# Mamba layers on one core: the residual add moved to POOL, the scan's DMA order and tile steps rearranged, and the layer norm's root issued later

## The chip, the cores and the metric
The kernel runs on one core of a Trainium2 chip. The metric is the device time of one execution in microseconds (us). Engines: PE (TensorE), DVE (VectorE), ACT (ScalarE), POOL (GpSimd), and SP, which only issues DMAs here.

## What is computed
Four layers are applied one after the other to x of shape (4, 1024, 512), float32. Layer 0 is softmax attention, layer 1 linear attention; the change leaves them alone. Layers 2 and 3 are Mamba blocks with a gate from the conditioning vector (layer 3 works on rows permuted by an index):

```python
xn = _layernorm(x, ln_g, ln_b) * (1.0 + scale[:, None, :]) + shift[:, None, :]
xz = xn @ in_proj.T                 # x_in and z, 1024 columns each
u  = silu(causal_conv4(x_in))
dt_r, B, C = split(u @ x_proj.T, [64, 80])
dt = softplus(dt_r @ dt_proj.T + dt_b)
h  = h * exp(dt_t * A) + (dt_t * u_t) * B_t      # for each time step t, 1024 x 16 states
y  = sum_n(h * C_t) + u * D
out = x + gate[:, None, :] * ((y * silu(z)) @ out_proj.T)
```

## The kernel before, in words
The program is one launch with a block for each stage; in a block each engine has its own queue, in an order written out by hand, and semaphores between the queues. Each of the two Mamba layers has two stages.

**ssm_inputs** handles the four batches in turn (loop `it`). For a batch PE makes the x products (8 tiles m of 128 channels), DVE does the convolution, ACT the silu; then come the x_proj product and its copy to SBUF by ACT (`proj_copy`), and then a loop over m = 0 to 7: PE makes one z product (z_with(m)) and DTP(m), DVE takes `relu(m)` of DTP, ACT its `Abs`. ACT works in two groups of four m: behind the fourth Abs of a group it loads the table of Exp, does four Exp, loads the table of Ln and does four Ln; DVE's `finish_dt(m)` needs the Ln. Between the groups, at m = 4, PE makes four more z products (Z_MID), and behind each of them `turn_rows(it + 1, ...)`: four transposes of the next batch's centered rows. These rows are centered by DVE (`rows.center`, eight steps, a semaphore after the fourth and the eighth), which waits for `rows.root` on ACT: Ln and Exp of the variances, on a 128x8 tile. DVE's queue has relu(0) to relu(3), center(it + 1), finish_dt(0), finish_dt(1), relu(4), finish_dt(2), ... PE uses a ring of four PSUM banks for z products and turned rows, which ACT empties (`take_z` with silu, `take_rows`).

**scan** runs over 64 blocks: 4 batches x 2 halves of 512 time steps x 8 channel tiles m. A block has 8 units of two states n; a unit k is two DVE scans (`recur`), with `h` held in a ring of three groups of four units. Around a unit:
- PE `make_drive(k + 4)` makes the input terms, ACT `lay(k + 4)` copies them into h;
- ACT `decay(k)` makes exp(dt * A) for both states, DVE `recur(k)` scans;
- POOL `multiply(k)` multiplies the two states by C, held in Crep (16 states x 512 steps, in four quarters of 1 MB; one buffer, reloaded at each change of half);
- PE `turn(k - 2)` transposes and sums over states into y; behind a block's last unit the u * D term follows, then DVE `gate` multiplies by silu(z) in zg, and SP stores it to scratch g.

The output products of 32 tiles of 128 rows are woven in, 16 units per tile, a half behind the scan: `tile_at(k)` gives the tile and the step within it. PE transposes g (`turn_g`, two parts, from og), ACT copies (`copy_g`), PE makes 8 `product`s into the bank O, DVE `gate_o` multiplies by the gate; in layer 2 a second DVE instruction adds the residual x. Layer 3 has residual None and adds it later, in gather_add. O, og, o and x have one buffer each.

SP's queue issues, per block, the loads of uD, dT, B, z, dt, og, x, gt and the stores of g and o, each with its wait. At the last block of a half (m = 7) it also reloads Crep: `load_C(half, q)` waits until POOL has done 2q + 2 units of that block.

In the code below these names stand as they are; a first half (th = 0) starts its scans from zero, a second half (th = 1) from `carry`.

## Time and profile before

| | us |
|---|---|
| median of 3 runs | 7161.26 (7154.28 to 7166.18) |
| the profiled execution, its own time | 7161.26 |
| its span, first to last instruction | 7159.3 |
| ssm_inputs of layer 2 / scan of layer 2 | about 2850 to 3600 / 3605 to 4975 |
| ssm_inputs of layer 3 / scan of layer 3 | about 4975 to 5730 / 5730 to 7078 |

Times in rows are microseconds from the span's start unless marked ns. A row of a timeline has the start, the duration, the engine, the line of the kernel, the operation and out<-in; x8 means eight merged instructions, and the bracket tells how long the engine was idle before and what released it. Instructions on one engine overlap a little, so a pitch is read from start to start.

### The profile page before, as it was taken

To read this page: it belongs to the slowest core of one execution; us is meant where nothing else is said; L and a number is where in the kernel's file an instruction comes from. 1 tells how busy PE (TensorE), PEld (TensorE's weight loads), DVE (VectorE), ACT (ScalarE), POOL (GpSimd) and SP (SyncE) were. 2 spreads that over 40 slices of the span, in tenths; PEclk is the share of its full clock that TensorE was granted. 3 is DMA by queue.
4 is the path that set the end of the run, shared out by engine and by line. 5 is a ranking of instruction groups with operands and counts; after the bars stand their busy time and mean duration, and the time that the engine had idled before them with its cause. 6 is when DMAs were issued, how large, how long until landed. Compare 5 with 4: busy or idle time off the path is not lost. (4 is left out here: it accounts for less than half of the span.)

```text
span 7159.3 us, 89203 instructions
## 1 busy us (share of the span) xinstructions
PE 5975.5 (83%) x31488; PEld 4036.9 (56%) x31488; DVE 5018.3 (70%) x6369; ACT 4537.6 (63%) x6817; POOL 2482.0 (35%) x1098
## 2 busy tenths in 40 slices
PE   6989999999889757988858888886888768888883
PEld 2448888888634343434356666663344356666661
DVE  2459999999642244454489999994454489999992
ACT  1228888888621142444479889993455489999991
POOL 0000000000000000000079999993000089999993
PEclk9999999999989878999889999998999889999996
DMA  5442222222242244233356666553233456655554
GB/s 196 170 150 60 72 63 74 66 72 60 87 147 97 111 148 173 87 140 132 149 147 164 166 159 159 155 157 100 99 135 129 152 148 167 159 154 156 151 146 169
DMA packets 608855, 935.18 MB, mean 131 GB/s; under 512 B 104984, under 2 KB 252568, under 8 KB 607908
## 3 DMA queue, kind: packets, MB, share of 16 engines
q1 hardware_dynamic: 596964, 904.27, 42.0%
q0 software_dynamic: 5120, 16.78, 0.7%
q10 hardware_dynamic: 6336, 8.52, 0.3%
q8 instruction: 249, 4.08, 0.2%
q14 instruction: 186, 1.52, 0.1%
HBM read 590.40 MB, written 338.98 MB: 130 GB/s over the span
## 5 line engine op out<-in xcount | busy, mean ns | idle before, releaser
L1609 POOL TENSOR_TENSOR scan_hC<-scan_h,scan_Crep 128x1024 f32<-128x1024 f32 x1024 | 2395.0, 2376 | 2880.7 <-DVE scan_h L1776 2856.2
L1720 ACT ACTIVATE scan_a<-scan_dt,scan_A 128x512 f32<-128x512 f32 x2048 | 1371.1, 696 | 117.7 <-DVE scan_h L1776 94.1
L1643 PE MATMUL scan_y<-ident,scan_hC 128*128 128x128 f32 x8192 | 1116.3, 280 | 384.1 <-POOL scan_hC L1609 383.1
L1643 PEld LDWEIGHTS scan_y<-ident,scan_hC 128*128 128x128 f32 x8192 | 902.7, 142 | 781.1 <-POOL scan_hC L1609 705.7
L1776 DVE TENSOR_TENSOR_SCAN scan_h<-scan_a,scan_carry,scan_h 128x512 f32<-128x512 f32 x1024 | 1214.6, 1260 | 13.7 <-ACT scan_a L1720 13.7
L1776 DVE TENSOR_TENSOR_SCAN scan_h<-scan_a,scan_h 128x512 f32<-128x512 f32 x1024 | 1155.3, 1200 | 55.8 <-ACT scan_a L1720 53.4
L1696 ACT COPY scan_h<-scan_drive 128x1024 f32<-128x1024 f32 x1024 | 1040.8, 1016 | 146.8 <-PE scan_drive L1631 137.1
L1631 PE MATMUL scan_drive<-scan_Bd,scan_dT 128*128 128x256 f32 x4096 | 751.8, 306 | 117.0 <-ACT scan_h L1696 57.6
L805 DVE TENSOR_TENSOR att_pTlo<-att_TP,att_pThi 128x512 fp32r<-128x512 f32 x1024 | 657.9, 684 | 128.1 <-ACT att_pThi L843 126.3
L843 ACT CAST att_pThi<-att_TP 128x512 fp32r<-128x512 f32 x1024 | 547.8, 587 | 179.7 <-PE att_TP L738 172.5
L1631 PEld LDWEIGHTS scan_drive<-scan_Bd,scan_dT 128*128 128x128 f32 x4096 | 560.0, 193 | 163.5 <-issue 78.1
L798 DVE CUSTOM_DVE_ANT_0 att_sm<-att_S,att_mneg 128x1024 f32<-128x1024 f32 x512 | 622.0, 1215 | 12.3 <-POOL att_mneg L716 12.1
L858 ACT ACTIVATE att_pr<-att_sm,att_nmax 128x1024 f32<-128x1024 f32 x512 | 592.4, 1157 | 45.9 <-DVE att_nmax L798 45.9
L738 PE MATMUL att_TP<-ident,att_pr 128*128 128x128 f32 x4096 | 564.9, 278 | 25.0 <-DVE att_pTlo L805 24.8
L497 PE MATMUL p_bank<-p_W,p_xT 128*128 128x512 f32 x1280 | 566.6, 599 | 5.1 <-ACT p_xT L395 5.1
L738 PEld LDWEIGHTS att_TP<-ident,att_pr 128*128 128x128 f32 x4096 | 452.4, 141 | 184.8 <-issue 116.8
L746 PE MATMUL att_YT<-att_pThi,att_v 128*64 128x256 f32 x2048 | 538.5, 298 | 0.0
L1669 PE MATMUL scan_O<-scan_Wo,scan_gT 128*128 128x512 f32 x1024 | 533.6, 614 | 5.4 <-ACT scan_gT L1727 5.4
L1205 PE MATMUL ssmin_ring<-ssmin_Wz,ssmin_xT 128*128 128x512 f32 x1024 | 476.4, 614 | 46.9 <-ACT ssmin_zt L1275 46.9
L746 PE MATMUL att_YT<-att_pTlo,att_v 128*64 128x256 f32 x2048 | 496.5, 277 | 0.0
L716 POOL TENSOR_SCALAR att_mneg<-att_mrow 128x1024 f32<-128x1024 f32 x4 | 14.5, 3636 | 1267.1 <-DMA att_mrow<-mask 1267.1
L1205 PE MATMUL ssmin_ring<-ssmin_xT,ssmin_Wx 128*128 128x512 f32 x1024 | 452.9, 598 | 0.0
(151 smaller groups left out, 6828.6 us busy)
## 6 DMA issues: line engine op xcount, KB each, us to landing
scan_dT<-scratch_dtuT SPq DMA_DIRECT2D x512, 256.0 KB, 5.5
scratch_dtuT<-ssmin_dT SPq DMA_DIRECT2D x128, 512.0 KB, 2.9
scan_Crep<-scratch_bc SPq DMA_DIRECT2D x64, 1024.0 KB, 9.6
att_q<-scratch_q_split SPq DMA_DIRECT2D x256, 128.0 KB, 3.0
att_k<-scratch_k_split SPq DMA_DIRECT2D x256, 128.0 KB, 3.2
scratch_uD<-ssmin_uD SPq DMA_DIRECT2D x64, 512.0 KB, 4.4
scratch_z<-ssmin_zt SPq DMA_DIRECT2D x128, 256.0 KB, 2.0
scratch_dt<-ssmin_dt SPq DMA_DIRECT2D x64, 512.0 KB, 2.6
```

The costliest lines, as they stand in the source:

```text
L738: last = nc.tensor.transpose(TP[:, m * P:(m + 1) * P], pr[u % 2][:, m * P:(m + 1) * P], ident[:])
L746: last = nc.tensor.matmul(YT[:, pair * 2 % 4:pair * 2 % 4 + 2, :], v[n // 4 % 2][:, m, n % 4, :].bitcast(F32R), pT[part][pair % 2][:, :, m ...
L798: nc.vector.tensor_tensor_reduce(sm[u % 2][:], S[u % 2][:], mneg[b % 2][:], -1.0, HUGE, ALU.add, ALU.min, nmax[u % 2][:]).then_inc(s["shif ...
L805: nc.vector.tensor_tensor(pT[1][u // 2 % 2][:, u % 2, cols_].bitcast(F32R), TP[:, cols_], pT[0][u // 2 % 2][:, u % 2, cols_], ALU.subtract ...
L858: nc.scalar.activation(pr[u % 2][:], sm[u % 2][:], ACT.Exp, bias=nmax[u % 2][:, 0:1], scale=-1.0, accum_out=psums[:, at:at + 1]).then_inc( ...
L1205: last = nc.tensor.matmul(ring[e % 4][:], lhs, rhs, start=(kt == 0), stop=(kt == KT - 1))
L1609: nc.gpsimd.tensor_tensor(hC[k % 2][:], of, Crep[:, 2 * p:2 * p + 2, :], ALU.mult).then_inc(s["scaled"].handle, 1)
L1631: last = nc.tensor.matmul(drive[:, c * TC:(c + 1) * TC, :], dT[j][:, at * P:(at + 1) * P].bitcast(F32R), Bd[th][:, at, :, first:first + GS ...
L1643: last = nc.tensor.matmul(y[j][:, t, :], hC[k % 2][:, i, t * P:(t + 1) * P], ident[:], start=(p == 0 and i == 0 and t == 0), stop=False, i ...
L1696: nc.scalar.copy(h[group % 3][:, :, tt * P:(tt + 1) * P], drive[:].rearrange("p t n -> p n t")).then_inc(s["laid"].handle, 1)
L1720: nc.scalar.activation(a[(2 * k + i) % 3][:], dt[j][:], ACT.Exp, scale=A[:, m, 2 * p + i:2 * p + i + 1]).then_inc(s["decayed"].handle, 1)
L1776: nc.vector.tensor_tensor_scan(of, a[(2 * k + i) % 3][:], of, first, ALU.mult, ALU.add).then_inc(s["scanned"].handle, 1)
```

## The change
In ssm_inputs, `rows.root(act, it + 1)` moves from behind proj_copy to behind the first group's Ln. In scan:
- the residual add of layer 2 moves from DVE (out of PSUM) to POOL (from o and x, both in SBUF), with a semaphore o_added;
- the tile's steps: start 4 units into the half instead of 8; turn_g's second part at step 5 (was 4), the products at 7 to 14 (were 6 to 13), gate_o at 15 (was 13); the loops end earlier;
- in PE's queue, turn(k - 2) comes ahead of turn_g and product of the same k;
- SP's order: load_C's four quarters all go last in the block of m = 7, x and the first part of og go behind z in odd blocks, the o store and og's second part into even blocks, around z.

```diff
                 nc.scalar.copy(xd[:], X[0:R + 2 * NS, :]).then_inc(c["proj_copy"].handle, 1)
-                if it + 1 < B:
-                    rows.root(act, it + 1)
                 for group in (range(0, 4), range(4, 8)):
                     if group[0] == 4:
+                        if it + 1 < B:
+                            rows.root(act, it + 1)
                         for n in Z_MID:
                             take_z(n)
...
-            n = (k - HALF_UNITS - UNITS) // 16
-            return (n, (k - HALF_UNITS - UNITS) % 16) if 0 <= n < TILES else (None, None)
+            n = (k - HALF_UNITS - 4) // 16
+            return (n, (k - HALF_UNITS - 4) % 16) if 0 <= n < TILES else (None, None)
...
             def load_C(half, q):
                 b, th = half // 2, half % 2
-                if half:
-                    w(sp, "scaled", half * HALF_UNITS - UNITS + 2 * q + 2)
...
-            for blk in range(BLOCKS + IB + 2):
+            for blk in range(BLOCKS + IB + 1):
                 half, m = blk // IB + 1, blk % IB
-                tile = (blk - IB - 1) // 2
+                tile = (blk - IB) // 2
                 if blk < BLOCKS:
                     load_uD(blk)
-                if m % 2 == 1 and 0 <= tile < TILES:
-                    load_og(tile, 1)
-                    if tile % TT == 0:
-                        load_gt(tile)
-                if m % 2 == 1 and 1 <= tile <= TILES:
-                    store_o(tile - 1)
-                if m % 2 == 0 and 0 <= tile < TILES and residual is not None:
-                    load_x(tile)
-                change = half < 2 * B and m == IB - 1
-                if change:
-                    load_C(half, 0)
                 if blk + 2 < BLOCKS:
                     load_dT(blk + 2)
-                if change:
-                    load_C(half, 1)
                 if half < 2 * B and 1 <= m <= 4:
                     load_B(half, range(8 * (m - 1), 8 * m))
                 if 1 <= blk <= BLOCKS:
                     store_g(blk - 1)
...
+                if m % 2 == 0 and 1 <= tile <= TILES:
+                    store_o(tile - 1)
                 if blk < BLOCKS:
                     load_z(blk)
-                if change:
-                    load_C(half, 2)
-                if m % 2 == 1 and 0 <= tile + 1 < TILES:
-                    load_og(tile + 1, 0)
+                if m % 2 == 0 and 0 <= tile < TILES:
+                    load_og(tile, 1)
+                if m % 2 == 1:
+                    if 0 <= tile < TILES:
+                        if tile % TT == 0:
+                            load_gt(tile)
+                        if residual is not None:
+                            load_x(tile)
+                    if 0 <= tile + 1 < TILES:
+                        load_og(tile + 1, 0)
                 if blk + 2 < BLOCKS:
                     load_dt(blk + 2)
-                if change:
-                    load_C(half, 3)
+                if half < 2 * B and m == IB - 1:
+                    for q in range(4):
+                        w(sp, "scaled", blk * UNITS + 2 * q + 2)
+                        load_C(half, q)
...
+            def add_residual(n):
+                w(pool, "o_gated", n + 1)
+                pool.wait_ge(x_in.handle, x_in.at(16 * (n + 1)))
+                nc.gpsimd.tensor_tensor(o[:], o[:], x[:], ALU.add).then_inc(s["o_added"].handle, 1)
+
+            for k in range(UNITS_ALL + HALF_UNITS + 8):
+                if k < UNITS_ALL:
+                    multiply(k)
+                n, step = tile_at(k - 2)
+                if residual is not None and step == 15:
+                    add_residual(n)
...
                 if k + 4 < UNITS_ALL:
                     make_drive(k + 4)
+                if 0 <= k - 2 < UNITS_ALL:
+                    turn(k - 2)
                 n, step = tile_at(k)
                 if step == 1:
                     turn_g(n, 0)
-                if step == 4:
+                if step == 5:
                     turn_g(n, 1)
-                if step is not None and 6 <= step < 14:
-                    product(n, step - 6)
-                if 0 <= k - 2 < UNITS_ALL:
-                    turn(k - 2)
+                if step is not None and 7 <= step < 15:
+                    product(n, step - 7)
...
-                if residual is None:
-                    nc.vector.tensor_tensor(o[:], O[:], gt[:], ALU.mult).then_inc(s["o_gated"].handle, 1)
-                else:
-                    nc.vector.tensor_tensor(O[:], O[:], gt[:], ALU.mult).then_inc(core.vector_step.handle, 1)
-                    dve.wait_ge(core.vector_step.handle, core.vector_step.at(n + 1))
-                    dve.wait_ge(x_in.handle, x_in.at(16 * (n + 1)))
-                    nc.vector.tensor_tensor(o[:], O[:], x[:], ALU.add).then_inc(s["o_gated"].handle, 1)
+                nc.vector.tensor_tensor(o[:], O[:], gt[:], ALU.mult).then_inc(s["o_gated"].handle, 1)
...
                 n, step = tile_at(k - 1)
-                if step == 13:
+                if step == 15:
                     gate_o(n)
```
On ACT copy_g's second part moves from step 5 to step 6.

## Rows read from the trace of the kernel before

**Rows 1.** Busy time by window; columns PE, PEld, DVE, ACT, POOL, PEclk, DMA share, GB/s
```profile
3640.00:4895.00 1255.00, 1027.96 (x6923) 806.60 (x6923) 1225.74 (x1123) 1135.12 (x1623) 1175.57 (x504) 0.99 0.58 154
...
4990.00:5725.00 735.00, 631.93 (x1696) 289.81 (x1696) 340.74 (x389) 351.13 (x434) 23.29 (x24) 0.91 0.35 127
```

**Rows 2.** Timeline of ACT, ssm_inputs of layer 3, batch 0
```profile
5093.41 0.30 ACT L367 ACTIVATE ssmin_lv<-ssmin_mv,eps 128x8 f32<-128x8 f32 x1
5093.73 1.28 ACT L370 ACT_TABLE_LOAD   x1
5095.02 0.21 ACT L370 ACTIVATE ssmin_rstd<-ssmin_lv 128x8 f32<-128x8 f32 x1
...
5115.06 1.11 ACT L1320 ACTIVATE ssmin_ea<-ssmin_DTP,column_tables 128x1024 f32<-128x1024 f32 x1 [2.71 <-DVE ssmin_dt L1380]
...
5126.98 1.28 ACT L1275 ACT_TABLE_LOAD   x1
```

**Rows 3.** Timeline of PE, the same stretch
```profile
5117.10 0.60 PE L387 MATMUL ssmin_ring<-ident,ssmin_x 128*128 128x128 f32 x4
5117.53 3.60 PE L1205 MATMUL ssmin_ring<-ssmin_Wz,ssmin_xT 128*128 128x512 f32 x8
5120.97 0.60 PE L387 MATMUL ssmin_ring<-ident,ssmin_x 128*128 128x128 f32 x4
5128.92 6.12 PE L1205 MATMUL ssmin_ring<-ssmin_Wz,ssmin_xT 128*128 128x512 f32 x8 [7.36 <-ACT ssmin_zt L1275]
...
5143.15 1.98 PE L1238 MATMUL ssmin_DTP<-ssmin_xd,ssmin_Wdt 64*128 64x512 f32 x4
```

**Rows 4.** Timeline of DVE, the same stretch
```profile
5114.94 3.73 DVE L377 TENSOR_SCALAR ssmin_x<-ssmin_x,ssmin_mv,ssmin_rstd 128x512 f32<-128x512 f32 x8
```

**Rows 5.** Groups by line, 4990 to 5725: busy us, mean ns, idle before
```profile
L1205 PE MATMUL ssmin_ring<-ssmin_Wz,ssmin_xT 128*128 128x512 f32 x512 | 238.4, 614 | 23.4 <-ACT ssmin_zt L1275 23.4
```

**Rows 6.** Timeline of DVE, gate_o of successive tiles, in three stretches of the scans
```profile
4028.06 0.67 DVE L1761 TENSOR_TENSOR scan_O<-scan_O,scan_gt 128x512 f32<-128x512 f32 x1
...
4066.46 0.68 DVE L1761 TENSOR_TENSOR scan_O<-scan_O,scan_gt 128x512 f32<-128x512 f32 x1
...
4149.49 0.68 DVE L1761 TENSOR_TENSOR scan_O<-scan_O,scan_gt 128x512 f32<-128x512 f32 x1
...
4189.62 0.67 DVE L1761 TENSOR_TENSOR scan_O<-scan_O,scan_gt 128x512 f32<-128x512 f32 x1
...
6118.40 0.67 DVE L1759 TENSOR_TENSOR scan_o<-scan_O,scan_gt 128x512 f32<-128x512 f32 x1
...
6156.07 0.67 DVE L1759 TENSOR_TENSOR scan_o<-scan_O,scan_gt 128x512 f32<-128x512 f32 x1
```

**Rows 7.** Timeline of POOL, a first half of layer 2
```profile
3969.16 23.28 POOL L1609 TENSOR_TENSOR scan_hC<-scan_h,scan_Crep 128x1024 f32<-128x1024 f32 x10 [0.38 <-DVE scan_h L1776]
```

**Rows 8.** Waits in the scans: us in total, times, longest; layer 2 twice, then layer 3
```profile
DVE scan_o L1764 <- DMA scan_x<-scratch_x: 17.9, 6, 3.8
...
DVE scan_h L1776 <- ACT scan_a L1720: 9.6, 8, 1.9
...
DVE scan_h L1776 <- ACT scan_a L1720: 13.8, 10, 3.2
```

**Rows 9.** SP's issue of dt in a block; then all landings of Crep
```profile
4066.24 0.33 SPq L1504 DMA_DIRECT2D scan_dt<-scratch_dt  x1
...
DMA to landing us min/median/max: 5.8/9.6/14.3
```

**Rows 10.** Timeline of POOL and DVE behind a change of half, layer 3
```profile
6705.94 6.97 POOL L1609 TENSOR_TENSOR scan_hC<-scan_h,scan_Crep 128x1024 f32<-128x1024 f32 x3 [3.13 <-DMA scan_Crep<-scratch_bc]
...
6713.06 2.34 DVE L1776 TENSOR_TENSOR_SCAN scan_h<-scan_a,scan_h 128x512 f32<-128x512 f32 x2 [3.19 <-ACT scan_a L1720]
6717.21 4.57 DVE L1776 TENSOR_TENSOR_SCAN scan_h<-scan_a,scan_h 128x512 f32<-128x512 f32 x4 [1.81 <-ACT scan_a L1720]
```

**Rows 11.** Timeline of PE behind the last scan of layer 2
```profile
4900.85 3.60 PE L1669 MATMUL scan_O<-scan_Wo,scan_gT 128*128 128x512 f32 x8
```

More of the change, by code:

```diff
@@ L1456, in scan @@
                                                   "y_full", "gated", "A_in")}
-        s.update({"o_" + n: core.count("out_" + n) for n in ("turned", "copied", "made", "gated")})
+        s.update({"o_" + n: core.count("out_" + n) for n in ("turned", "copied", "made", "gated", "added")})
         crep_in = core.slot_in[0:4]
@@ L1465, in scan @@
         where = lambda blk: (blk // (2 * IB), blk // IB % 2, blk % IB)
+        o_done = s["o_gated" if residual is None else "o_added"]
         def tile_at(k):
-            n = (k - HALF_UNITS - UNITS) // 16
-            return (n, (k - HALF_UNITS - UNITS) % 16) if 0 <= n < TILES else (None, None)
+            n = (k - HALF_UNITS - 4) // 16
+            return (n, (k - HALF_UNITS - 4) % 16) if 0 <= n < TILES else (None, None)
         block = ctx.enter_context(nc.Block())
@@ L1534, in load_x @@
                 if n >= 1:
-                    w(sp, "o_gated", n)
+                    w(sp, "o_added", n)
                 sp.dma_start(x[:], residual[n // TT, n % TT * P:(n % TT + 1) * P, :]).then_inc(x_in.handle, 16)
@@ L1544, in store_o @@
             def store_o(n):
-                w(sp, "o_gated", n + 1)
+                sp.wait_ge(o_done.handle, o_done.at(n + 1))
                 sp.dma_start(dst[n // TT, n % TT * P:(n % TT + 1) * P, :], o[:]).then_inc(o_out.handle, 16)
@@ L1610, in multiply @@
                                         ).then_inc(s["scaled"].handle, 1)
-            for k in range(UNITS_ALL):
-                multiply(k)
+            def add_residual(n):
[8 more added lines that the diff above has]
+                    add_residual(n)
         @block.tensor
@@ L1674, in _ @@
                 make_drive(n)
-            for k in range(UNITS_ALL + HALF_UNITS + UNITS + 2):
+            for k in range(UNITS_ALL + HALF_UNITS + 8):
                 if k + 4 < UNITS_ALL:
                     make_drive(k + 4)
+                if 0 <= k - 2 < UNITS_ALL:
+                    turn(k - 2)
                 n, step = tile_at(k)
@@ L1731, in _ @@
                 lay(n)
-            for k in range(UNITS_ALL + HALF_UNITS + UNITS + 2):
+            for k in range(UNITS_ALL + HALF_UNITS + 8):
                 if k < UNITS_ALL:
@@ L1741, in _ @@
                     copy_g(n, 0)
-                if step == 5:
+                if step == 6:
                     copy_g(n, 1)
@@ L1782, in _ @@
                                       ).then_inc(s["cleared"].handle, 1)
-            for k in range(UNITS_ALL + HALF_UNITS + UNITS + 2):
+            for k in range(UNITS_ALL + HALF_UNITS + 8):
                 if k < UNITS_ALL:
@@ L1800, in scan @@
     if residual is not None:
-        core.vector_step.stage_added(TILES)
+        s["o_added"].stage_added(TILES)
         x_in.stage_added(16 * TILES)
```

## The prediction
> **What bounds the kernel now.** I read the busy time by stage first [rows 1]. In layer 2's scan DVE is busy for 1225.74 of 1255 us (98%) and POOL for 1175.57 (94%). In the stage ahead of layer 3's scan, which prepares its inputs, no engine is full: PE has 631.93 of 735 us. So in a scan what DVE does sets the time and POOL is 4% behind it, while in the input stage one must look at which wait ends last. For that I read the ACT and PE timelines of one batch's middle, then the tiles' pitch on DVE in the scans, then the waits and SP's issues where the scan changes half.
>
> **The change, part by part**, against the profiled execution (span 7159.3, time 7161.26, which is also the median of the three runs; the 2 us between them stay).
>
> *1. rows.root moved behind the first Exp/Ln group.* Today ACT does the root (Ln, table load, Exp) right after proj_copy and is through at 5095.2 [rows 2]. It costs nothing there: PE's Z products wait nowhere but in the stall below (0 otherwise [rows 5]), and ACT's fourth Abs (5115.06) waits 2.71 us on DVE's relu, not on ACT's own earlier work [rows 2]. So leaving it out there gains nothing. In its new place it starts at 5126.98, where the next silu table load starts today. Ln needs no new table (Ln has just run): 0.30; table load 1.28; Exp 0.21: root done at 5128.8 instead of 5095.2; the silu table then comes at 5130.1, in time for a ring bank that PE needs only after its next product. On DVE, center is queued ahead of finish_dt(0); today it starts at 5114.94 and does 8 steps in 3.73 us [rows 4]. Then it starts at 5128.85, and its first four steps (the first half, which PE waits for) end about 1.95 us later, at 5130.8. PE has turn_rows(it+1, 0) queued directly behind the first Z_MID product; today it runs at 5117.10, the second product at 5117.53 and its turn at 5120.97, all under ACT's Exp/Ln [rows 3]. Afterwards PE stands at the first turn until 5130.8, and those three come behind it.
> Today from the end of that stall (5128.92) to DTP(4) (5143.15) are 14.23 us, with third and fourth Z_MID products, z_with(4) and their turns, the first product at a fallen clock (6.12 us instead of 3.60). After the change a turn (0.43), a product (3.44) and a turn (0.43) come ahead of these 14.23, all from 5130.85 on: 5130.85 + 4.30 + 14.23 = 5149.38, so 6.23 us later. All after DTP(4) (relu and Abs of m = 4 to 7, second Exp/Ln, finish_dt, next batch's x products) hangs on it: nothing in that chain has spare work to hide it. The stall today occurs three times in the layer (23.4 us [rows 5]), that is once for each batch with a root behind it, and 2 x 3 = 6 in the kernel: 6 x 6.23 = **+37.4**. Bounds: 33 (if PE's restart costs a little less) to 46 (if the doubled idle time, 13.6 us instead of 7.36, makes it restart 1.4 us slower).
> The Trainium skill (ScalarE: Activation LUTs, section "Table sets: the hidden batching unit") has Ln and Exp in one common set, so that Exp behind Ln needs no load. Here the trace disagrees: a load of 1.28 us stands between them [rows 2]. By the rule each root would end 1.28 us earlier and the part would come to +29.7.
>
> *2. The residual add moves from DVE to POOL (layer 2 alone).* Tile pitch on DVE in a first half (scan from zero) is 4066.46 - 4028.06 = 38.40 us, in a second half 40.13; layer 3, which has no add, has 37.66 in a first half [rows 6]. So DVE gains 38.40 - 37.66 = 0.74 us per tile. POOL does ten multiplies in 23.28 us [rows 7], a pitch of (23.28 - 2.36) / 9 = 2.32, or 37.2 per tile of 16. An add of 128x512 on POOL stands nowhere in the trace; the nearest row is this multiply of twice the size, 2.36 us. Upper end 2.36 (no less for half the size), lower 0.69 (DVE's own add, as layer 3's lack of it shows 0.74); I take half the multiply, 1.18, plus a little: 1.2. In first halves POOL then needs 38.4, as much as today's DVE pitch, so the 12 tiles there gain nothing (+0.2 each for the uneven load: 2.4). In second halves DVE keeps 39.39 against POOL's 38.4 to 38.8, but the add delays the multiply behind it by 1.1 us and PE, ACT and DVE are linked tightly (three units of scan between a multiply and the scan that its turn lets go), so I give 0.45 back: -0.29 x 15 tiles = -4.4. Sum **-2**; with 0.69: -17; with 2.36: +14.
> The Trainium skill (GPSIMD Engine Reference, section "3.1 Elementwise — side-by-side cycle accounting") gives 4497 ns for a two-input add of 2048 elements. An estimate from that page with the 2.36 of this trace for 1024 puts 512 elements at 1.3 us; it would add about 1.2 us to the sum.
>
> *3. SP's order: the four Crep loads go last, x goes earlier.* Today DVE waits 17.9 us for x in six tiles, all behind a change of half, because x sits behind Crep; DVE also waits 9.6 us (layer 2) and 13.8 us (layer 3) for scan_a, nearly all just behind changes, where a late Crep or og held PE [rows 8]. The new order issues z, x and og ahead of Crep. If all of it goes: 17.9 + 9.6 + 13.8 = **-41**.
> The price: the first Crep quarter used to go out six units of scan ahead of its use. Now it stands behind load_dt(blk+2), which waits for the block's last decay. Such an issue stands at 4066.24, 0.2 us before the end of the seventh scan unit (4066.46) [rows 6, 9]. With one unit (2.3) left in the block, dt goes out 2.5 us and Crep 2.0 us ahead of the new half; POOL needs it one unit in, 4.3 us after issue. Landings of Crep are 5.8 at least, 9.6 in the middle, 14.3 at most [rows 9]; the 5.8 belongs to a load at the head of a burst, as here, but with up to 1 MB of z, x, og and dt just ahead of it. I take 6.7: POOL stalls 2.4. In the trace a POOL stall of 3.13 on Crep makes DVE lose 3.19, and 1.81 more four units on [rows 10]; in the new PE order a product stands between turn and the next drive, so there is less slack. I price 2.4 at 2.3 of DVE: seven changes in each scan, 14 x 2.3 = **+32**. Bounds: 1.5 of stall, most of it absorbed, 14 x 0.8 = 11; the middle landing 9.6, stall 5.3, 14 x 5 = 70. The later quarters then have room: POOL uses one per 4.6 us.
>
> *4. PE's order and the tile's steps.* turn now precedes the tile's transposes and products, so a product (3.60 / 4 = 0.9 us [rows 11]) lies in the chain turn, drive, lay, decay. In second halves, with 0.1 us more per unit (pitch 39.4 against 37.7 for 16), this fits; in first halves I take 0.15 us for each of layer 3's 12 tiles: **+2** (0 to 6).
>
> *5. The tail.* Four products of tile 27 (3.60 us) follow the last turn today [rows 11]; two would, so the O bank is free 1.8 us earlier. In layer 2 the store ahead of og waits for POOL's add (+0.3 on each of four tiles, +0.6 on the last). Together **-1.5** (-4 to +3).
>
> Sum: 37.4 - 2 - 41 + 32 + 2 - 1.5 = +26.9, so 7161.3 + 26.9 = **7188**.
>
> **The rivals.**
> *A. The Crep burst lands in time* (not slower). POOL would stall no more than today; the point that decides is a landing of 4.3 us or less after issue, or a slack that absorbs the stall. Then the 32 go: 7156. For it: the landing of 5.8 is only 1.5 us over that point. Against: no Crep load of the trace landed below 5.8.
> *B. root's move is hidden*: PE would have other work or the late batch would be caught up before the next one. Then the 37.4 go: 7151. Against: PE's queue is in order, and the stall at 5128.92 is on the one chain that leads to DTP(4).
> *C. The burst is worse than its head*: Crep quarters queue behind each other and behind dT, landings come near the middle of the rows (9.6), and DVE loses 5 per change: 26.9 + 38 = +65, 7226. For it: the 14.3 us landing belongs to the third load of a burst. Against: a first load of a burst landed in 5.8.
> *D. POOL becomes the bound of layer 2*: an add of 2.36 us, +16 over the sum: 7204. For it: POOL has 1.2 us per tile to spare in first halves, no more. Against: multiply's time is mostly elements.
> *E. Exp needs no load behind Ln* (the rule cited in part 1): the root ends 1.28 us earlier six times: 7180. Against: today's load between the two.
>
> **How the numbers follow.** Chances: the forecast 0.60, A 0.13, B 0.06, C 0.11, D 0.08, E 0.02. The time is the forecast's, 7188; its own range is 7172 to 7206. The 8-in-10 range leaves out the far part of C, where 14 x 5 applies at every change, and what lies beyond A and B together: 7152 to 7224. A measurement of this kernel tells 0.2% (14 us) from no change, that is 7147 and 7175.6. Faster: A and B at once, or either with a cheap add: 0.08. Same: the rest of A, B and the low edge of the forecast (0.06 of it): 0.17. Slower: 0.75.
>
> **What would show it.** In the changed profile: PE's wait ahead of the first turn_rows of the next batch should appear at about 13 us, on DVE's center, six times, and the 7.36 us wait on the silu should be gone; the input stages should each be 19 us longer. No x wait on DVE; 32 POOL adds of about 1.2 us; POOL's waits on Crep at the first unit of each half, about 2 us each, 14 times; tile pitch in layer 2 near 38.4 and 39.7. I would be wrong if center ran before the Exp/Ln group, if Crep landed in under 4.5 us or its quarters queued, or if the add took over 1.5 us.

## The result and the profile after

| | us |
|---|---|
| the changed kernel, median of 4 runs | 7287.30 (7279.52 to 7292.78) |
| the kernel before, median of 4 runs beside it | 7158.04 (7154.28 to 7166.18) |
| ratio, with its 95% interval | 1.0178 (1.0161 to 1.0196) |
| profiled execution, its own time / span | 7276.74 / 7274.9 |

The change makes the kernel 1.8% slower, 127 us by ratio. The prediction had the sign right and the size wrong: 7188, with 7224 as its upper end. In the profiled executions the 115.6 us between the spans lie here. A scan is taken from the start of its first DVE scan to the start of its last; an input stage from its first root, or from the end of layer 2's last o, to the first scan; a tail from there to the end of the layer's last o.

| stretch | before | after | difference | forecast |
|---|---|---|---|---|
| ssm_inputs of layer 2 | 760.7 | 780.6 | +19.8 | +18.7 |
| scan of layer 2 | 1276.2 | 1323.0 | +46.8 | about -13 |
| ssm_inputs of layer 3 | 785.7 | 805.2 | +19.5 | +18.7 |
| scan of layer 3 | 1243.5 | 1280.7 | +37.2 | about +4 |
| the two tails | 149.6 | 146.6 | -3.0 | -1.5 |

What lies ahead of layer 2's inputs and behind layer 3's last o, which the change doesn't touch, is 4.0 and 0.7 us shorter. So the input stages came as forecast and the scans did not. First the windows, as in [rows 1] (busy time of PE, PEld, DVE, ACT, POOL, then the clock):

```profile
3656.00:4940.00 1284.00, 1044.60 (x6840) 834.04 (x6840) 1200.06 (x1081) 1119.90 (x1607) 1190.39 (x524) 0.97 0.56 149
5070.00:5800.00 730.00, 625.19 (x1662) 283.67 (x1660) 329.17 (x360) 336.30 (x417) 23.27 (x24) 0.92 0.34 123
```
In layer 2's scan DVE is busy for 93% of the time, before for 98%: it is less full and yet the stage is longer. No engine became the bound by its work (POOL 93%); the engines wait for each other.

**The input stage.** ACT, then PE, in the stretch that answers to [rows 2, 3], and last PE's first Z_MID product before:

```profile
5189.09 1.28 ACT L370 ACT_TABLE_LOAD   x1
```
```profile
5175.48 3.70 PE L1205 MATMUL ssmin_ring<-ssmin_Wz,ssmin_xT 128*128 128x512 f32 x8
5192.69 1.08 PE L387 MATMUL ssmin_ring<-ident,ssmin_x 128*128 128x128 f32 x4 [13.50 <-DVE ssmin_x L377]
5193.56 4.74 PE L1205 MATMUL ssmin_ring<-ssmin_Wz,ssmin_xT 128*128 128x512 f32 x8
...
5210.29 1.98 PE L1238 MATMUL ssmin_DTP<-ssmin_xd,ssmin_Wdt 64*128 64x512 f32 x4
```
```profile
5113.56 3.70 PE L1205 MATMUL ssmin_ring<-ssmin_Wz,ssmin_xT 128*128 128x512 f32 x8
```
The first Z_MID product stands 61.92 us later than before (5113.56). From there the turn comes at 5130.77 on the old time (forecast 5130.85), after a wait of 13.50 on center in place of the 7.36 on the silu table, and DTP(4) 5.22 us later than before (forecast 6.23; the product behind the stall took 4.74, not 6.12). Another 0.86 us comes at PE's next restart after an idle time (its sixteen products take 8.73 us, before 7.88). That is 6.1 us for this batch; the layer's other two batches with a root behind them lose 6.6 and 6.8. The wait of 13.50 stands there in all six. The table load between Ln and Exp is there (1.28).

**The scans.** DVE's gate_o in successive tiles, as in [rows 6]: a first and a second half of layer 2, then of layer 3:

```profile
4346.79 0.68 DVE L1763 TENSOR_TENSOR scan_o<-scan_O,scan_gt 128x512 f32<-128x512 f32 x1
4387.76 0.68 DVE L1763 TENSOR_TENSOR scan_o<-scan_O,scan_gt 128x512 f32<-128x512 f32 x1
...
4139.75 0.68 DVE L1763 TENSOR_TENSOR scan_o<-scan_O,scan_gt 128x512 f32<-128x512 f32 x1
4180.79 0.68 DVE L1763 TENSOR_TENSOR scan_o<-scan_O,scan_gt 128x512 f32<-128x512 f32 x1
...
6205.64 0.68 DVE L1763 TENSOR_TENSOR scan_o<-scan_O,scan_gt 128x512 f32<-128x512 f32 x1
6244.68 0.68 DVE L1763 TENSOR_TENSOR scan_o<-scan_O,scan_gt 128x512 f32<-128x512 f32 x1
...
6367.35 0.68 DVE L1763 TENSOR_TENSOR scan_o<-scan_O,scan_gt 128x512 f32<-128x512 f32 x1
6407.24 0.68 DVE L1763 TENSOR_TENSOR scan_o<-scan_O,scan_gt 128x512 f32<-128x512 f32 x1
```
Before, in a second half of layer 3:
```profile
5963.40 0.67 DVE L1759 TENSOR_TENSOR scan_o<-scan_O,scan_gt 128x512 f32<-128x512 f32 x1
6002.79 0.67 DVE L1759 TENSOR_TENSOR scan_o<-scan_O,scan_gt 128x512 f32<-128x512 f32 x1
```
The pitch is 40.97 and 41.04 in layer 2 (before 38.40 and 40.13) and 39.04 and 39.89 in layer 3 (before 37.67 and 39.39). Over 12 tiles in first and 15 in second halves that is 31 + 14 + 16 + 7 = 68 us. The scans are 84 us longer; the 16 that are left lie where the scan changes half.

The 40.97 is not the pitch of every first-half tile of layer 2. Here are two of them from gate_o to gate_o, with columns as in [rows 1], the third from the right being the granted clock of PE:
```profile
4346.79:4387.76 40.97, 35.13 (x226) 28.06 (x225) 37.99 (x36) 36.33 (x55) 38.52 (x18) 0.96 0.51 131
4641.54:4681.79 40.25, 33.31 (x221) 26.05 (x220) 38.00 (x37) 36.42 (x55) 38.48 (x18) 1.00 0.58 148
```
Away from the changes of half, a tile in a first half of layer 2 has 40.24 to 40.27 where the granted clock was 1.00 and 40.9 to 41.1 where it was 0.96. So some 0.7 us of the 2.57 go with the clock and 1.9 do not. Over layer 2's whole scan the mean granted clock is 0.97, before 0.98.

The add and all landings of Crep, as in [rows 9]:

```profile
L1611 POOL TENSOR_TENSOR scan_o<-scan_o,scan_x x32: 1262/1276/1291, 3850.0 to 5033.8; 128x512 f32<-128x512 f32 x32
```
```profile
  DMA scan_Crep<-scratch_bc: 34.8, 14
...
DMA to landing us min/median/max: 6.1/10.9/18.1
```
The same wait of POOL before:
```profile
  DMA scan_Crep<-scratch_bc: 17.2, 14
```
Both are as priced: an add of 1.28 us, and POOL waits for Crep 14 times for 2.49 (forecast 2.4). Fourteen waits alone would prove little, since before there were 14 too, of 1.2 us; but all of those stood at the third or fourth quarter, and now 13 of the 14 stand at the first quarter of a new half, as forecast. That quarter lands 6.6 to 7.7 us behind its issue (forecast 6.7). The next two do queue behind it, 9.3 to 11.2 and 12.4 to 14.4 us behind theirs, but POOL's only other wait for Crep is 0.2 us. DVE has no wait for x any more. What is new stands in the waits of layer 2's scan, of after and of before:

```profile
ACT scan_h L1701 <- PE scan_drive L1636: 133.0, 153, 6.4
...
DVE scan_h L1775 <- ACT scan_a L1725: 82.4, 65, 5.8
```
```profile
ACT scan_h L1696 <- PE scan_drive L1631: 36.0, 64, 2.9
```
ACT's lay waits for the drive in 153 units instead of 64, and behind it DVE for scan_a 82.4 us instead of 9.6 [rows 8]. So the first theory was PE's order; rivals were the steps and the add.

### The profile page after: what moved, and what is told of

Its sections match the earlier page's. It is cut to its first block and busy times, and to the rows that moved or that the text cites. A ratio compares the mean times of both kernels' runs of the same rounds, so it can differ in the third digit from the quotient of the medians.

```text
span 7274.9 us, 89191 instructions
## 1 busy us (share of the span) xinstructions
PE 6039.8 (83%) x31488; PEld 4103.6 (56%) x31488; DVE 5012.1 (69%) x6337; ACT 4517.0 (62%) x6805; POOL 2521.1 (35%) x1130
## 3 DMA queue, kind: packets, MB, share of 16 engines
q1 hardware_dynamic: 596964, 904.27, 41.1%
## 5 line engine op out<-in xcount | busy, mean ns | idle before, releaser
L1648 PE MATMUL scan_y<-ident,scan_hC 128*128 128x128 f32 x8192 | 1139.6, 283 | 369.5 <-POOL scan_hC L1605 364.5
L1725 ACT ACTIVATE scan_a<-scan_dt,scan_A 128x512 f32<-128x512 f32 x2048 | 1351.9, 694 | 48.6 <-DVE scan_h L1775 45.4
L1636 PE MATMUL scan_drive<-scan_Bd,scan_dT 128*128 128x256 f32 x4096 | 881.4, 338 | 139.6 <-ACT scan_h L1701 84.4
L1636 PEld LDWEIGHTS scan_drive<-scan_Bd,scan_dT 128*128 128x128 f32 x4096 | 600.9, 195 | 414.1 <-issue 249.2
## 6 DMA issues: line engine op xcount, KB each, us to landing
scan_Crep<-scratch_bc SPq DMA_DIRECT2D x64, 1024.0 KB, 10.9
```

Source lines behind the costliest of these rows:

```text
L1636: last = nc.tensor.matmul(drive[:, c * TC:(c + 1) * TC, :], dT[j][:, at * P:(at + 1) * P].bitcast(F32R), Bd[th][:, at, :, first:first + GS ...
L1648: last = nc.tensor.matmul(y[j][:, t, :], hC[k % 2][:, i, t * P:(t + 1) * P], ident[:], start=(p == 0 and i == 0 and t == 0), stop=False, i ...
L1725: nc.scalar.activation(a[(2 * k + i) % 3][:], dt[j][:], ACT.Exp, scale=A[:, m, 2 * p + i:2 * p + i + 1]).then_inc(s["decayed"].handle, 1)
```

## The experiments

All ratios below are to the kernel before on the same chip, with half-intervals of 0.0009 to 0.0019; 0.0014 is 10 us. So a difference between two of these runs is uncertain by 10 to 20 us. "Given back" is counted against the changed kernel.

**One edit undone at a time.** e1 puts turn(k - 2) behind product again, e2 the steps (start at 8 units, second turn_g at 4, products at 6, gate_o and POOL's add at 13), e3 the add, e4 the root.

```diff
# e1
-                if 0 <= k - 2 < UNITS_ALL:
-                    turn(k - 2)
                 n, step = tile_at(k)
...
                     product(n, step - 7)
+                if 0 <= k - 2 < UNITS_ALL:
+                    turn(k - 2)
# e2
-            n = (k - HALF_UNITS - 4) // 16
+            n = (k - HALF_UNITS - UNITS) // 16
...
```

> The changed kernel with one edit undone: in PE's queue turn(k - 2) stands behind turn_g and product again. Theory 1: the tile's pitch grew by 2.57 us (layer 2, first halves, 12 tiles), 0.91 (15 tiles), 1.37 and 0.49 (layer 3), 68 us in all, because each product now lies in the chain turn, drive, lay, decay, scan: ACT's lay waits for the drive in 154 units of layer 2 instead of 65. Then undoing the order gives back 30 to 50 us (time 7237 to 7257), and layer 3's pitch returns to 37.7 and 39.4. Theory 2: the steps are the cause (the gate_o of a tile now falls on the same unit as the block's gate with silu(z), and the first part of the tile on other units). Then this run stays within 10 us of the changed kernel (7277 to 7290) and layer 3's pitch stays at 39.0. Theory 3: it is the add on POOL; then layer 3 has no part in it, and layer 2's pitch of 40.97 stays.

> The changed kernel with the tile's steps undone (start 8 units into the half, second turn_g at 4, products at 6 to 13, gate_o and POOL's add at 13), PE's order and all else as changed. Theory 1 (PE's order is the cause): within 10 us of the changed kernel, 7277 to 7297, the pitch in layer 3's first halves still near 39.0. Theory 2 (the steps are, gate_o and gate on the same unit): 20 to 50 us are given back, 7237 to 7267, and layer 3's pitch falls under 38.2.

> The changed kernel with the residual add back on DVE (two instructions, out of PSUM), all else as changed. Theory 3 (POOL's add of 1.28 us starves the scan of layer 2): 25 to 40 us are given back, 7247 to 7262, and layer 2's pitch falls from 40.97 and 41.04 to under 39.8 and 40.5. Theory 1 (PE's order): DVE has 0.7 us more work per tile but the loss by POOL goes, so between -10 and +10 us, 7277 to 7297. My prediction had it at +2, because it priced the move at -2.

> The changed kernel with rows.root(act, it + 1) back behind proj_copy, all else as changed. The input stages of both layers are 38.7 us longer in the changed profile (19.8 and 18.9); the theory that root's place makes all of it expects 37 to 40 given back, 7247 to 7250, PE's wait for center (85.8 us of DVE for rstd in 8 times) gone and the stall of 7.4 on the silu table back. Rival: part of the 38.7 came from elsewhere (the scan that ends differently, or code loading), then under 30 are given back, above 7257.

| run | median us | ratio |
|---|---|---|
| e1, PE's order undone | 7293.05 | 1.0197 |
| e2, steps undone | 7245.63 | 1.0131 |
| e3, add undone | 7255.73 | 1.0145 |
| e4, root undone | 7236.49 | 1.0116 |

e4: input stages 761.4 and 784.7, 19.2 and 20.5 us shorter, spans 40.9 apart: the root's place makes all of term 1. The median lies 10 us below the expectation's 7247 to 7250, and by ratio 44 us come back. (The 18.9 in the expectation ran from the start of the last o before and from its end after; end to end it is 19.5.)

e1 refutes the plain form of theory 1: no time came back. Yet its pitch in layer 3's first halves is 37.85, as it said, so something else ate it. The PE and SP timelines behind a change of half in e1 show what:

```profile
6181.14 0.71 PE L1636 MATMUL scan_drive<-scan_Bd,scan_dT 128*128 128x256 f32 x4
6186.69 1.11 PE L1666 MATMUL scan_O<-ident,scan_og 128*128 128x128 f32 x4 [4.83 <-DMA scan_og<-scratch_g]
6187.60 1.91 PE L1648 MATMUL scan_y<-ident,scan_hC 128*128 128x128 f32 x8
```
```profile
6183.11 0.37 SPq L1515 DMA_DIRECT2D scan_zg<-scratch_z  x1
6183.58 0.45 SPq L1529 DMA_DIRECT2D scan_og<-scratch_g  x1
```
The new SP order loads og's second part behind z, and the new steps ask for it three units earlier (start 4 and step 5, before 8 and 4); with turn queued behind turn_g, PE stands 4.83 us at og and the scan with it (31.8 us in 7 times in layer 3; 2.4 in the changed kernel). So the change needs its PE order as a guard against its own late og. e6 below completes the square: with the old steps PE's new order costs 57 us (e2 against e6), with the new steps it costs nothing that can be told (the changed kernel against e1, -14); the new steps cost 104 us with PE's old order (e1 against e6) and 34 with the new one.

e2 and e3 both give much back (34 and 24 us by ratio), and both chiefly in layer 2 (scan 1288.8 and 1297.3 against 1323.0). e3 is what theory 3 said in time and nearly in pitch (39.76 and 40.61 in layer 2). e2 is what theory 2 said in time, but layer 3's pitch stays at 38.85 and doesn't fall under 38.2. No single theory says both: the parts interact.

**Parts alone.** e5 has only PE's order changed in the kernel before; e6 is the changed kernel with steps and PE's order undone; e7 is the kernel before with SP's new order; e8 the changed kernel with Crep's four loads issued at their old places:

```diff
# e8
                 if blk < BLOCKS:
                     load_uD(blk)
...
+                if change:
+                    crep(0)
                 if blk + 2 < BLOCKS:
                     load_dT(blk + 2)
+                if change:
+                    crep(1)
...
-                if half < 2 * B and m == IB - 1:
-                    for q in range(4):
-                        w(sp, "scaled", blk * UNITS + 2 * q + 2)
-                        load_C(half, q)
...
```

> The kernel before with one edit of the change: in PE's queue turn(k - 2) ahead of turn_g and product of the same k. The run with the order undone (e1_pe_order) gave no time back, but its pitch in layer 3's first halves was 37.85 against 39.03, and what it won there it lost in a wait of PE for og (31.8 us in 7 times in layer 3). Theory: the order itself costs pitch, and in the kernel before, where og comes in time, nothing is won for it: layer 3's pitch goes from 37.67 to 38.85 and from 39.40 to 39.88 (12 x 1.2 + 15 x 0.5 = 22 us), layer 2's from 38.4 and 40.13 by 0.3 to 1.2: together 25 to 45 us, 7180 to 7200. Rival: pitch grows only together with the add on POOL or the new steps: within 5 us of the kernel before, 7150 to 7160.

> The changed kernel with the tile's steps and PE's order both undone; root's place, the add on POOL and SP's order stay. With the steps undone alone it took 7245.6. Theory (product in the chain is the cause of the rest of the pitch): layer 3's pitch falls from 38.85 to 37.7 and from 39.88 to 39.4 (22 us), layer 2's from 39.4 to about 38.6 and 40.0 to 39.6 (16 us), and og, asked for later now, comes in time: 7200 to 7215. Rival: the wait for og that took the gain in e1_pe_order comes here too, 14 times 4 us: above 7240.

> The kernel before with SP's new order as its only edit (Crep's four quarters last in the block of m = 7, x and og earlier). My prediction: x and scan_a waits go (-41), POOL stalls 2.4 in 14 changes at 2.3 of DVE each (+32): -9, about 7146. Theory from the changed kernel, where the changes of half together cost 2 us more than before in layer 2 and 13 more in layer 3: +15, about 7170. Second theory: part of those 15 comes from the early steps or PE's order, then between: 7150 to 7160.

> The changed kernel with the four loads of Crep issued where the kernel before has them (around dT and z, the last behind dt), all else as changed. Theory: POOL's waits for Crep (34.8 us in 14 changes) and the 3 to 4.5 us that DVE loses behind each go: 25 to 45 us given back, 7245 to 7262. Rival: z, og and x come behind 1 MB loads again, and PE or DVE wait for these instead: within 10 us of the changed kernel, 7277 to 7297.

| run | median us | ratio |
|---|---|---|
| e5, before + PE's order | 7202.93 | 1.0071 |
| e6, changed - steps - PE's order | 7197.45 | 1.0052 |
| e7, before + SP's order | 7145.70 | 0.9981 |
| e8, changed, Crep early | 7257.45 | 1.0141 |

e5: PE's order alone costs 0.7% or 51 us, with nothing else changed, a little more than the 25 to 45 expected; the rival is out. PE in a first half of layer 3, first before, then e5:

```profile
6133.11 1.09 PE L1643 MATMUL scan_y<-ident,scan_hC 128*128 128x128 f32 x8 [0.36 <-POOL scan_hC L1609]
...
6137.22 1.02 PE L1669 MATMUL scan_O<-scan_Wo,scan_gT 128*128 128x512 f32 x2
6138.08 1.04 PE L1643 MATMUL scan_y<-ident,scan_hC 128*128 128x128 f32 x8
6138.87 0.72 PE L1631 MATMUL scan_drive<-scan_Bd,scan_dT 128*128 128x256 f32 x4
```
```profile
6166.38 1.09 PE L1643 MATMUL scan_y<-ident,scan_hC 128*128 128x128 f32 x8 [0.30 <-POOL scan_hC L1609]
6167.31 1.02 PE L1669 MATMUL scan_O<-scan_Wo,scan_gT 128*128 128x512 f32 x2
6167.77 1.03 PE L1631 MATMUL scan_drive<-scan_Bd,scan_dT 128*128 128x256 f32 x4
```
Before, a unit without a product has PE wait 0.36 us for POOL's multiply ahead of turn (6133.11). In a unit with one the product runs at that time, PE doesn't wait, and the drive follows the turn at once. In e5 PE first waits for POOL, then turns, then makes the product, and the drive ends later by the product and takes 1.03 instead of 0.72; ACT's lay waits 0.51 for it in the next unit (6168.89 of its timeline).

e6 lands at 37 us over before by its ratio (interval 24 to 50). The prediction's sum without parts 4 and 5 is +26: so the miss is in the steps, PE's order and what these do to the other parts, as far as an interval of 26 us can tell. e7 refutes the +15 and agrees with the prediction's -9 (measured -14): DVE waits 16.0 and 16.2 us for scan_a in the two scans and never for x, 32.2 in place of 41.3, where -41 and +32 were forecast. e8 is as expected (-26 us by ratio): POOL's Crep waits fall from 34.8 to 4.7, DVE's gain is partly lost to og (PE waits 13.4 and 14.0 us for it in the two scans; 4.9 and 2.4 in the changed kernel).

**The start at unit 4, and PE's order split.** e9 starts a tile at 6 units, all else as changed; e10 lets PE do product, turn, turn_g.

```diff
# e9
-            n = (k - HALF_UNITS - 4) // 16
+            n = (k - HALF_UNITS - 6) // 16
...
# e10
+                if step is not None and 7 <= step < 15:
+                    product(n, step - 7)
                 if 0 <= k - 2 < UNITS_ALL:
                     turn(k - 2)
...
-                if step is not None and 7 <= step < 15:
-                    product(n, step - 7)
```

> The changed kernel with a tile starting 6 units into the half instead of 4; steps, PE's order, the add on POOL and all else as changed. Now gate_o comes two units behind the block's gate with silu(z), as in the kernel before, while at 4 both fall on the same unit (k = 4 modulo 8), with POOL's add right behind. Pitch of layer 2 in the changed kernel 40.97 and 41.04, with the old steps 39.4 and 40.0, with the new steps and the add on DVE 39.76 and 40.61. Theory: both gates on one unit and the add behind them make the difference: pitch 39.4 to 39.6 and 40.0 to 40.2 in layer 2, 38.85 in layer 3, 25 to 40 us given back in all, 7247 to 7262. Rival: it is the inner steps (second turn_g, products and copy_g one or two units later): pitch stays at 40.9 and 41.0, 7275 to 7297.

> The changed kernel with PE's order product, turn(k - 2), turn_g in place of turn, turn_g, product; all else as changed. Theory: the product ran in the shadow of PE's wait for POOL ahead of turn in the kernel before; behind turn it delays the next drive by 0.9 us and ACT's lay with it (133 us of waits in 154 units of layer 2 against 36 in 65), which makes 1.2 us of pitch; and the turn ahead of turn_g keeps a late og from holding the scan (the loss of e1_pe_order: 31.8 us of PE in 7 times). With this order both are had: layer 3's pitch 37.7 to 37.9 and 39.4 to 39.6, no wait of DVE over 5 us behind a change of half; 25 to 40 us given back, 7247 to 7262. Rival: the og wait comes back since a product needs the copy of turn_g's result a unit later, then 7280 to 7300; second rival: the pitch comes from turn_g too, then under 15 us given back.

e9: 7221.59, ratio 1.0098: 57 us given back, more than expected, since layer 3 gains too (pitch 38.23 and 39.61). Layer 2 has 39.40 and 40.01, as said. DVE and POOL at the end of a tile, first in the changed kernel, then in e9:

```profile
4180.21 0.67 DVE L1755 TENSOR_TENSOR scan_zg<-scan_y,scan_zg 128x512 f32<-128x512 f32 x1
4180.79 0.68 DVE L1763 TENSOR_TENSOR scan_o<-scan_O,scan_gt 128x512 f32<-128x512 f32 x1
4181.39 14.30 DVE L1775 TENSOR_TENSOR_SCAN scan_h<-scan_a,scan_carry,scan_h 128x512 f32<-128x512 f32 x12
4196.90 2.46 DVE L1775 TENSOR_TENSOR_SCAN scan_h<-scan_a,scan_carry,scan_h 128x512 f32<-128x512 f32 x2 [1.22 <-ACT scan_a L1725]
```
```profile
4183.91 2.35 POOL L1605 TENSOR_TENSOR scan_hC<-scan_h,scan_Crep 128x1024 f32<-128x1024 f32 x1 [1.17 <-PE scan_y L1648]
4186.23 1.27 POOL L1611 TENSOR_TENSOR scan_o<-scan_o,scan_x 128x512 f32<-128x512 f32 x1
```
```profile
4189.87 1.09 PE L1648 MATMUL scan_y<-ident,scan_hC 128*128 128x128 f32 x8 [1.99 <-POOL scan_hC L1605]
```
```profile
4170.14 0.67 DVE L1763 TENSOR_TENSOR scan_o<-scan_O,scan_gt 128x512 f32<-128x512 f32 x1
4170.72 14.39 DVE L1775 TENSOR_TENSOR_SCAN scan_h<-scan_a,scan_carry,scan_h 128x512 f32<-128x512 f32 x12
4185.03 0.67 DVE L1755 TENSOR_TENSOR scan_zg<-scan_y,scan_zg 128x512 f32<-128x512 f32 x1
4185.82 4.81 DVE L1775 TENSOR_TENSOR_SCAN scan_h<-scan_a,scan_carry,scan_h 128x512 f32<-128x512 f32 x4
```
With 4, both gates fall on one unit; POOL, which has just lost 1.17 us to a late turn, does the add, PE's turn waits 1.99 for it, and 1.22 reach DVE. A wait like this, 1.2 us or more, stands behind the gates in every tile of layer 2; in first halves POOL has lost its 0.9 to 1.0 us to DVE and not to a turn. With 6 a dozen scans lie between the gates, and DVE goes on without a bracket, although PE's turn behind the add still waits 1.64 us. That the offset decides is shown; which of its coincidences (two gates together, the add behind a late turn, turn_g beside the block's last turn) weighs most is argued only. The granted clock is a part of it that no run separates: in layer 2's scan its mean is 0.99 in e9 and e2 and 0.97 in the changed kernel.

e9 and e2 have gate_o on the same unit of a block, and e9 is faster by some 24 us. So the later steps inside a tile don't harm; the start at 4 does.

e10: 7255.50, ratio 1.0145, 24 us given back: the theory's time, but pitch 38.28 and 39.67 in layer 3, not 37.7. Products are some two thirds of what the order costs there (39.04 to 38.28 of 39.04 to 37.85), turn_g behind turn the rest; and POOL still waits for late turns (24.9 us in layer 2).

**Toward a faster kernel.** e11 is the kernel before with SP's new order but Crep's loads as early as before; e12 adds the add on POOL to it; e13 is the kernel before with that add alone; e14 is e12 with the store of o moved in SP's queue:

```diff
# e14
                     load_uD(blk)
+                if m % 2 == 1 and 1 <= tile <= TILES:
+                    store_o(tile - 1)
...
-                if m % 2 == 0 and 1 <= tile <= TILES:
-                    store_o(tile - 1)
```

> The kernel before with SP's new order for x, og, gt and the o store, but the four loads of Crep at their old places: no other edit. The run with the whole new order (e7_sp_order_alone) was at 0.9981 of before, with POOL waits for Crep of 33.9 us in 13 times and DVE waits for scan_a of 32.2 us in both layers beyond the first fill. Theory: Crep's late issue costs nearly all of these, so 15 to 30 us less than e7: 7115 to 7130, a ratio of 0.994 to 0.996. Rival: og and x stand behind Crep again and their waits come back: between e7 and the kernel before, 7145 to 7160.

> The fastest version so far (e11_sp_crep_early, 7120 us: SP's new order with Crep's loads where they were) with the residual add on POOL in place of DVE. Theory (the add by itself is worth what the pitch says: 38.40 to 38.56 in first halves, 40.13 to 39.60 in second ones, as e6_steps_and_pe_order had them): 12 x 0.16 - 16 x 0.53 = -6.5, about 7114. Rival: POOL, with the add at 38.4 us of work in a tile of 38.56, can't catch up with any late load, and each of the seven changes of half costs 1 to 3 us more: 7120 to 7135. My prediction's number for this part is -2.

> The kernel before with the residual add on POOL as its only edit. My prediction: -2 (-17 to +14), and the x waits of DVE (17.9 us) become waits of POOL. Theory 3 of the first experiments (the add is what harms) would put it at +20 or more, 7175 and above; the theory that it harms only together with PE's new order and the start at unit 4 puts it at -10 to +8, 7143 to 7166.

> e12_crep_early_add (7143.6) with one thing moved in SP's queue: the store of o goes back from ahead of z in even blocks to behind uD in odd blocks. In e12 SP stands at that store until POOL's add is done (issued at 4072.78), and z, og, dt and then Crep bunch up behind it; POOL waits 25.4 us for Crep in layer 2 against 4.0 with the add on DVE. Theory: this makes the whole difference between e11 and e12; then Crep's waits fall under 10 us, the pitch stays 38.56 and 39.60, and the time is 7110 to 7122, a ratio of 0.9943 to 0.996. Rival: POOL has no slack (38.4 us of work in 38.56), the first late load costs as much as before: 7130 to 7145.

| run | median us | ratio |
|---|---|---|
| e11, before + SP's order, Crep early | 7120.05 | 0.9958 |
| e12, e11 + add on POOL | 7143.62 | 0.9984 |
| e13, before + add on POOL | 7132.77 | 0.9970 |
| e14, e12, o store later | 7118.10 | 0.9953 |

e13 refutes theory 3: the add alone makes the kernel 21 us faster. Its pitch is 38.56 and 39.60 (+0.16 and -0.53 a tile), -6 in sum, and the rest is the wait for x (17.9 us, [rows 8]): it is gone, since POOL asks for x a unit later than DVE did and never waits for it. With 21 us it lies below the 7143 that any theory had. e12 (7143.62) went the rival's way and beyond it (7120 to 7135), and e14 shows that its reason (a full POOL) was not the main one. SP in e12, SP in e14, then the waits of layer 2's scan in e12 and e14:

```profile
4072.78 0.34 SPq L1545 DMA_DIRECT2D scratch_x<-scan_o  x1
4073.16 0.43 SPq L1515 DMA_DIRECT2D scan_zg<-scratch_z  x1
...
4077.41 0.37 SPq L1486 DMA_DIRECT2D scan_Crep<-scratch_bc  x1
```
```profile
4058.81 0.38 SPq L1515 DMA_DIRECT2D scan_zg<-scratch_z  x1
...
4067.97 0.43 SPq L1545 DMA_DIRECT2D scratch_x<-scan_o  x1
```
```profile
POOL scan_hC L1615 <- DMA scan_Crep<-scratch_bc: 25.4, 12, 4.3
```
```profile
POOL scan_hC L1615 <- DMA scan_Crep<-scratch_bc: 13.1, 7, 2.3
```
In e12 z stands behind the store, which waits for POOL's add: z, og and dt go out in one bunch just ahead of Crep. Moved behind uD, the store holds z no more (4058.81, ahead of it), and 22 us come back. The expectation had them under 10. The 13.1 that stay (4.0 with the add on DVE, e11) may eat what the shorter pitch wins: e14 and e11 can't be told apart. Both beat the kernel before by 0.4 to 0.5%.

## Why the prediction was wrong

What each edit does to the pitch, from the runs that add one to the last (us per tile, first / second halves; SP's order alone, e7, leaves it as it was):

| | layer 2 | layer 3 | sum |
|---|---|---|---|
| before | 38.40 / 40.13 | 37.67 / 39.39 | |
| + add on POOL (e6, e13) | 38.56 / 39.60 | 37.67 / 39.39 | -6 |
| + PE's order (e2) | 39.40 / 40.01 | 38.85 / 39.88 | +38 |
| + the steps (changed) | 40.97 / 41.04 | 39.04 / 39.89 | +37 |

The last row's 40.97 holds for tiles at a granted clock of 0.96; at 1.00 it is 40.25.

- *Part 4 failed.* "In second halves ... this fits; in first halves I take 0.15 us for each of layer 3's 12 tiles: +2 (0 to 6)." In pitch it measures about +75, half order and half steps when they are added in the table's sequence. Two things were missed. The product was weighed against spare time per unit, when it had been free because it filled PE's wait for POOL's multiply; behind turn it lies on the way to the next drive in every half of both layers (e5: 38.84 to 38.87 and 39.88 in layer 3, where the second halves were said to have room), and layer 2 was given nothing at all. And the start at unit 4 was read as an earlier tile only; that 4 + 15 + 1 is 4 modulo 8, the unit of the block's own gate, can be read from the code, and it was missed.
- *Part 1 held*: +39.3 in the profiles (forecast 37.4), 40.9 of span in e4. It held with the load of 1.28 that its row showed. The Trainium skill (ScalarE: Activation LUTs, "Table sets: the hidden batching unit") has Ln and Exp in one shared set; the trace disagrees here too, with the load between them at 5189.09.
- *Part 2 had the sign right alone and the size too small*: -21 in e13 against -2, outside its bounds of -17 to +14. The pitch is -6 of it; the rest is the x wait, which the prediction had booked under part 3, and which either part removes. Its split (+0.2, -0.29) measured +0.16, -0.53. The add's 1.28 us is within the bounds taken from the rows. The estimate worked out from the Trainium skill (GPSIMD Engine Reference, "3.1 Elementwise — side-by-side cycle accounting"), 1.3 us, agrees with it. Missed was that with PE's order and the start at 4 the same add costs: the changed kernel loses 24 us by having it (e3).
- *Part 3 held alone and not in company*: alone -14 by ratio (-7 to -21), forecast -9, and 32.2 us of DVE waits in e7 against 32. POOL's 14 stalls are 2.49 against 2.4. Behind a stall DVE waits once, four units into the half: 0.6 to 4.1 us in e7, 2.3 in the mean, as priced; 1.7 to 4.5 in the changed kernel, 3.1 in the mean, and then again seven units later (0.2 to 5.8). So the changes of half cost 16 us in the changed kernel where this part had -9. These 25 us are the second largest piece of the miss behind part 4; that less slack is their reason is argued.
- *Part 5 held*: -3.0 against -1.5, nearly all of it in layer 3 (-2.9).
- *The rivals*: none happened. Crep landed neither in time (A) nor near 9.6 at its head (C: it was 6.6 to 7.7; the quarters behind it did queue, which the prediction named as a sign against itself, and it cost next to nothing), the root was not hidden (B), the add was not 2.36 (D), the load was there (E).
- *The range* summed bounds of single parts. Parts alone are +51 (e5), -14 (e7), -21 (e13) and about +44 (changed less e4), +60 together; the changed kernel has +127. Of the other 67 us some 18 are the x wait, which both e7 and e13 take away and which can go only once. The rest is the steps, which were never run alone on the kernel before, and interaction; no term had any room for these.

Open stays why the changed kernel's unprofiled runs have a median 10 us over its profiled one, where the kernel before has none; their mean granted clock is the same, 0.936 to 0.937. Open is also what of the steps' cost is the clock.

## What to carry to other kernels

Before an instruction is moved in an in-order queue, ask in whose wait it stands today: work that fills a wait is free only there. In a loop of woven periods (16 units of a tile, 8 of a block), write down modulo the shorter one where each extra instruction of every engine falls; here the start that put two gates on one unit cost 57 us (e9). Price parts together where they meet on engines that are over 90% busy: the add won 21 us alone and lost 24 in company. A store queued ahead of loads should not wait for a busy engine (22 us, e14). And look at the granted clock of a tile before you take its pitch as typical.

## What the runs showed of the hardware

- A drive (four matmuls of 256 columns) is recorded with 1.03 us right behind two product matmuls of 512 columns and with 0.72 behind transposes. It starts 0.46 behind the start of a product of 1.02, so the records overlap; that the extra 0.3 is time in PE's queue is my reading and wasn't tested.
- PE's first product after an idle time of 13.5 us took 4.74 us, with the transposes ahead of it 1.08 instead of 0.60; after 7.36 us of idle time, without them, it took 6.12 [rows 3]. The longer stall did not make this restart dearer. The granted clock was 0.60 in the 6.2 us from the start of the 6.12 product, and 0.72 in the 5.7 us from the start of the transposes behind 13.5 us.
- Crep's loads of 1 MB landed in 6.1 to 18.1 us (median 10.9) when the four are issued last in the block, against 5.8 to 14.3 (9.6) in the old order [rows 9].
- In the changed kernel PE idled 1.1 and 2.0 us around POOL's add in first-half tiles of layer 2, whether the granted clock of the tile was 1.00 or 0.96. In the tile of 40.97 us it fell behind these waits, to 0.67 in the 5.25 us from 4355.75 on, where eight transposes took 1.61 us instead of 1.09.
